# The start of a fused attention and expert layer on one core: where the first keys and queries are projected, rotated and moved, and in which order the first loads are issued

## The reference

```python
x = x + attention(layernorm(x), wq, wk, wv, wo)   # 32 heads of 64, 8 key/value heads, rotary, causal
x = x + experts(layernorm(x), gate, w0, w1, w2)   # 8 experts of width 512, the best 2 for each token
```

```python
q, k = rope(q), rope(k)                  # x * cos + rotate_half(x) * sin
probs = softmax(where(causal, q @ k.T / 8, min))
o = probs @ v
return o.reshape(b, s, NH * HD) @ wo.T
```

## Time and profile before

| | us |
|---|---|
| median of the runs | 823.74 (823.67 to 824.26, 3 runs) |
| the profiled execution | 824.96 |
| its span, first to last instruction | 823.0 |

### The profile page before, as it was taken

The page is one execution under the profiler, slowest core; times in us unless marked ns, Lnnn a source line. Parts: engine busy times, 40 slices in busy tenths (PEclk is TensorE's granted clock), DMA queues, the critical chain, the costliest instruction groups (busy, mean ns, idle before and its releaser), DMA issues.

```text
span 823.0 us, 19373 instructions
## 1 busy us (share of the span) xinstructions
PE 759.4 (92%) x5952; PEld 646.7 (79%) x5952; DVE 509.8 (62%) x2098; ACT 479.9 (58%) x1537; POOL 420.8 (51%) x674
## 2 busy tenths in 40 slices
PE   3689999999999999999999999986598999999994
PEld 2578887988888888889888888875477778888883
DVE  5788677767666757757766767776545754333331
ACT  2477876776777777677677777656244442222220
POOL 0456664656565555556465665542314454555442
PEclk9899999999999999999999999988999999999998
DMA  6432122212202302131221221218832222222330
GB/s 195 141 113 94 51 74 61 65 40 66 75 31 61 78 32 65 42 72 42 64 69 41 65 72 33 53 43 295 292 115 44 45 49 46 47 41 45 53 51 6
DMA packets 52851, 61.05 MB, mean 74 GB/s; under 512 B 10544, under 2 KB 45616, under 8 KB 52752
## 3 DMA queue, kind: packets, MB, share of 16 engines
q1 hardware_dynamic: 45264, 50.46, 21.1%
q0 software_dynamic: 7488, 9.36, 6.7%
HBM read 26.21 MB, written 9.32 MB: 43 GB/s over the span
## 4 chain that ended last, share of the span: by engine, by line
PE 76%; DVE 11%; ACT 5%; issue 4%; DMA 2%; SPq 1%; POOL 0%; POOLq 0%; DVEq 0%; ACTq 0%
PE h L1505 13%; PE projected L379 10%; PE attn_out L524 10%; PE probsT L484 9%; PE scores L471 8%; PE yb L1524 8%; PE heads_out L503 5%; PE projected L400 3%; PE heads_out L506 2%; PE tg L1515 2%; PE projected L357 2%; ACT exps L596 2%; ACT exps L594 1%; DMA raw<-w_attn 1%; PE tx L1497 1%
## 5 line engine op out<-in xcount | busy, mean ns | idle before, releaser
L898 POOL TENSOR_SCALAR probs<-exps,inv_sums 128x128 f32<-128x128 f32 x256 | 97.9, 382 | 227.8 <-DVE inv_sums L729 180.9
L603 ACT COPY pT<-probsT 128x384 f32<-128x384 f32 x256 | 121.7, 476 | 85.2 <-PE probsT L484 85.1
L484 PE MATMUL probsT<-identity,probs 128*128 128x128 f32 x768 | 132.1, 282 | 13.3 <-ACT pT L603 12.4
L594 ACT ACTIVATE exps<-masked,neg_max 128x128 f32<-128x128 f32 x256 | 102.8, 402 | 61.2 <-DVE neg_max L723 61.1
L596 ACT ACTIVATE exps<-masked,neg_max 128x256 f32<-128x256 f32 x256 | 127.2, 497 | 0.0
L899 POOL TENSOR_SCALAR probs<-exps,inv_sums 128x256 f32<-128x256 f32 x256 | 123.0, 480 | 0.0
L1715 POOL DMA_INDIRECT out<-y,to_token x39 | 61.9, 1586 | 110.8 <-DVE y L1645 90.8
L379 PE MATMUL projected<-xT_hi,w 128*128 128x256 f32 x512 | 112.7, 301 | 5.9 <-DVE k_sin L711 3.6
L1505 PE MATMUL h<-experts_w,xsT_hi 128*128 x312 | 108.9, 431 | 4.7 <-issue 3.3
L484 PEld LDWEIGHTS probsT<-identity,probs 128*128 128x128 f32 x768 | 88.9, 143 | 27.5 <-POOL probs L899 15.5
L723 DVE CUSTOM_DVE_ANT_0 masked<-scores,tables 128x256 f32<-128x256 f32 x256 | 107.5, 420 | 0.2 <-issue 0.2
(11 more groups left out here) (179 smaller groups left out, 1627.5 us busy)
## 6 DMA issues: line engine op xcount, KB each, us to landing
qT<-rotated SPq DMA_DIRECT2D x256, 64.0 KB, 2.1
kT<-k_cos SPq DMA_DIRECT2D x64, 128.0 KB, 3.3
experts_w<-w_in SPq DMA_DIRECT2D x16, 512.0 KB, 5.8
raw<-w_attn SPq DMA_DIRECT2D x20, 256.0 KB, 3.2
experts_w_out<-w_out SPq DMA_DIRECT2D x8, 512.0 KB, 7.1
out<-x_all SPq DMA_DIRECT2D x8, 256.0 KB, 2.3
xn_rows<-raw SPq DMA_DIRECT2D x8, 256.0 KB, 3.3
x_all<-x SPq DMA_DIRECT2D x1, 1792.0 KB, 11.4
```

The costliest lines, as they stand in the source:

```text
L484: mm = nc.tensor.transpose(p_bank[:, at:at + P], probs[:, h, at:at + P], ident[:, :])
L594: nc.scalar.activation(exps[:, h, 0:P], masked[:, h, 0:P], ACT.Exp, bias=neg_max[:, h, 0:1], scale=-1.0, accum_out=sums[:, h, 0:1])
L603: nc.scalar.copy(pT[:, n % 2, h, :], p_bank[:, 0:3 * P]).then_inc(pT_done, 1)
L898: nc.gpsimd.tensor_scalar(probs[:, h, 0:P], exps[:, h, 0:P], inv_sums[:, h, 0:1], 1.0, ALU.mult, ALU.mult)
```

## The change

- `project_q` and `rope_q` take the bank as an argument. The first turn's queries go to `y_bank`, the second's to `o_bank`; PE's waits for `k_parts` and `q_parts` between the first three projections go. The first `next_q` waits for `k_parts` in place of the second `q_parts`, since the keys are now what was last in `x_bank`.
- SP issues pieces 0 and 1 ahead of the tables. The four DMAs of the first keys leave SP for ACT (`move_first_keys`), between ACT's casts of pieces 3 and 4. SP moves the first queries before it loads pieces 4 and 5, not after.
- ACT casts piece 2 after `x_hi`, not before.
- DVE multiplies the first queries by the tables ahead of the split of piece 2; three (not four) tiles' statistics stand between that and the second queries, piece 3 is split right behind them, and eleven (not seven) tiles' statistics come after.
- PE multiplies the identity by itself, into `scores0`, whose content nobody reads: 9 times between the arrival of the identity and the transposes, 7 times between the transposes and the keys.

```diff
         sp.dma_start(ident[:, :], t["ident"]).then_inc(r["ident_in"], 16)
+        load_piece(0)
+        load_piece(1)
         sp.dma_start(tables[:, :], t["attn_consts"]).then_inc(consts_in, 16)
-        for i in range(SLOTS):
-            load_piece(i)
+        load_piece(2)
+        load_piece(3)
         sp.dma_start(x_all[:, TT:TILES, :], x_dram[:, TT:TILES, :]).then_inc(x_rest_in, 16)
-        move_k(0, 0)
+        move_q(0, 0, True)
         load_piece(SLOTS)
         load_piece(SLOTS + 1)
-        move_q(0, 0, True)
         move_q(1, 1, True)
...
-                    pe.wait_ge(q_parts, 2)
+                    pe.wait_ge(k_parts, 1)
...
+        def keep_busy(n):
+
+            for i in range(n):
+                nc.tensor.matmul(s_bank[0][:, 0:P], ident[:, :], ident[:, :], start=True, stop=True)
+
         pe.wait_ge(r["ident_in"], 16)
+        keep_busy(9)
         x_transposes(0)
+        keep_busy(7)
         project_k(0, 0)
-
-        pe.wait_ge(k_parts, 1)
-        project_q(0, 0)
-
-        pe.wait_ge(q_parts, 1)
-        project_q(0, 1)
+        project_q(0, 0, bank=y_bank)
+        project_q(0, 1, bank=o_bank)
...
-        for i in range(3):
-            split_w(i)
+        def move_first_keys():
+
+            act.wait_ge(k_rotated, 1)
+            for a in range(2):
+                for copy in range(2):
+                    at = copy * HD + a * 32
+                    act.dma_start(kT[at:at + 32, 0, :, :], k_cos[:, a, :]).then_inc(k_in[0], 16)
+
+        split_w(0)
+        split_w(1)
         x_hi(0)
+        split_w(2)
         split_w(3)
+        move_first_keys()
         split_w(4)
...
         rope_k(0, 0)
+        rope_q(0, True, y_bank)
         split_w(2)
 
         dve.wait_ge(x_rest_in, 16)
-        for i in range(TT, TT + 4):
+        for i in range(TT, TT + 3):
             nc.vector.bn_stats(stats[:, i, :], x_all[:, i, :])
-        rope_q(0, True)
-        for i in range(TT + 4, TT + 7):
+        rope_q(1, False, o_bank)
+        split_w(3)
+        for i in range(TT + 3, TT + 7):
             nc.vector.bn_stats(stats[:, i, :], x_all[:, i, :])
-        rope_q(1)
-        split_w(3)
         for i in range(TT + 7, TILES):
```

More of the change, by code:

```diff
@@ L366, in weights_split, with project_q @@
             return kept(kind, i)
-        def project_q(b, g, first=0, end=12):
+        def project_q(b, g, first=0, end=12, bank=x_bank):
             hi, lo = kept("q", g)
@@ L378, in project_q @@
                 at = k * 2 * P + a * P
-                mm = nc.tensor.matmul(x_bank[:, a * SEQ:(a + 1) * SEQ], part[:, at:at + P], x[:, b % 2, k, :],
+                mm = nc.tensor.matmul(bank[:, a * SEQ:(a + 1) * SEQ], part[:, at:at + P], x[:, b % 2, k, :],
                                       start=(i % 6 == 0), stop=(i % 6 == 5))
@@ L691, in x_lo, with rope_q @@
                                     xT_hi[:, b % 2, :, :].bitcast(F32), ALU.subtract).then_inc(xT_lo_done, 1)
-        def rope_q(m, first=False):
+        def rope_q(m, first=False, bank=x_bank):
             dve.wait_ge(q_ps, m + 1)
@@ L697, in rope_q @@
                 dve.wait_ge(q_rotated, m)
-            halves = x_bank[:, :].rearrange("p (a t) -> p a t", a=2)
+            halves = bank[:, :].rearrange("p (a t) -> p a t", a=2)
             nc.vector.tensor_tensor(by_cos[:, :, :], halves, cos, ALU.mult)
```

## The result

| | before | after |
|---|---|---|
| median of 12 runs, us | 823.70 (821.90 to 825.14) | 819.34 (815.56 to 821.54) |
| the profiled execution, us | 824.96 | 818.58 |
| its span, us | 823.0 | 816.7 |

The ratio of the runs is 0.9949, 95% interval 0.9934 to 0.9964: 4.2 us faster, by the interval 3.0 to 5.4 (the medians themselves are 4.4 apart). 819.3 had been forecast. The two profiled executions differ by more, 6.4 us, and the single runs of the changed kernel spread over 6 us. Part of both goes with TensorE's clock: of the twelve runs the fastest (815.56) had the highest mean granted clock, 0.982, and the three slowest (821.27, 821.27, 821.54) the lowest, 0.970. What else is in the spread isn't known, since a trace is kept of one run only.

The account below looks back on a forecast made before the run. PE bounds the later attention; at the start engines wait for one another, along DVE's path to first maxima and SP's to piece 6. Both meet 4.4 us earlier: 823.74 - 4.4 = 819.3 us median (820.5 profiled), range 817.0 to 822.4.

Parts of the forecast that it names:

- The two paths and where they meet: Start: DVE up to first maxima, SP up to piece 6; they meet at the third queries' rotation, 4.4 us earlier.
- The clock's rise: PE before the keys: unbroken work from 3.74 brings 2.4 GHz near 9.6, so keys begin at 10.7.
- The price of an identity product: PE around the transposes: 0.43 us each at 1.2 GHz (0.54 at most), 0.215 at 2.4 GHz.
- The x load: Big x load ahead of DVE's later statistics: keeps its place in the queue and lands by about 15.5.
- The landing of piece 6: Load that ACT casts before the second exponentials: issued at 23.15, landing at 25.95, 4.6 us earlier.
- The collision of DMAs: First queries' move sharing DMA engines with the keys' last DMA: nothing taken; scores at 21.1, 1.7 us later at no cost.
- Weights ahead of tables: First loads: pieces 0 and 1 there by 7 at the latest instead of 8.53, tables by 9.5.
- +/-1.5 for stretches at 1.2 GHz: Later slow-clock stretches, each some 1.5 us of PE, may vanish or appear; counted only in the range.
- rival C: Later 1.2 GHz stretches fall otherwise: one goes, 817.7 us, or one is added, 820.9; chance 0.10 each.
- Rival A: PE stays at 1.2 GHz because near-zero products don't raise the clock; 0.35 us later, 824.1; chance 0.06.
- Rival B: Clock falls in PE's gap before the second queries, which take 2.94 us, 1.2 more; 820.5 us; chance 0.15.
- Rival D: Keys' and queries' DMAs collide or issues are dear on ACT; 820.2 us, or 822.2 if transfers hold; chance 0.07.

Follow-up runs that it names:

- the fastest version: Changed kernel with piece 6 issued ahead of the second queries' DMAs and PE's waits filled with identity products; median 816.47 against 823.28 us, ratio 0.9922.
- the second set of runs: The changed kernel run again with no edit, for a second trace; median 820.10 against 823.60 us for the kernel before, ratio 0.9953.
- the first filled kernel: Changed kernel with more identity products in PE's waits (15, 12 and 4); median 817.63 us, ratio 0.9930 to the kernel before.
- that with nine products: Changed kernel without the seven identity products between transposes and keys, the nine ahead kept; ratio 0.9968 to the kernel before.
- one moved line: Changed kernel with SP issuing piece 6 ahead of the second queries' four DMAs, not behind; median 818.97 against 823.28 us, ratio 0.9942.
- the three kernels with filled waits: Changed kernel with extra identity products in PE's waits: alone (817.63 us), with piece 6 earlier (816.47), and that with keys' DMAs on SP (816.83).

## Why the prediction came out right, point by point

- *The two paths and where they meet* held. The chain went through piece 6, DVE was late next. First maxima were forecast for 24.25 and came at 23.17; piece 6 for 25.95 and was cast at 26.37; the third queries for 27.8 and came at 28.00. The sum was 4.4 for 4.20 and 4.04. That it fits so well is in part luck: 1.1 of the 4.4 are keys that begin at 10.7 and not at 11.80, and the 11.80 comes from the one late landing of piece 0 in the trace of before.
- *The clock's rise* was put near 9.6. It came by 7.8 in one trace and after 8.7 in the other, so the keys began at 9.90 and about 10.7. The price of an identity product, 0.215 at 2.4 GHz and 0.43 at 1.2, was right within the last one's tail (nine took 4.21 where the clock was 1.2 GHz throughout and 3.79 where it rose within them, seven 1.73). The sum there has a slip: with four of seven at 2.4 GHz the seven would end at 11.2; a rise at 9.6 leaves 5.7 of them at the higher level and gives the 10.8.
- *The x load* I had land by 15.5, with no one waiting. It landed at 15.9 and DVE waited 0.99 for it, which cost 0.2 at most, since the second queries were on PE until 16.7. The clock's early gain of 0.8 was still there when their rope began (16.93 for 17.75) and when SP issued piece 6 (22.46 for 23.15).
- *The landing of piece 6* was taken as 2.80, from one row. It took 3.88 in the first trace, and that is where the early gain went; in the second it took 2.85, after an issue 0.5 later than forecast. Two misses of opposite sign brought both traces to 28.0 and 28.16.
- *The collision of DMAs*, priced at nothing with 1.7 us of slack, cost about 0.9: the first queries were issued at 16.11, 0.8 ahead of the forecast, and the scores began 5.09 after that and not 4.15, at 21.20, where 21.1 was forecast. The slack covered it.
- *Weights ahead of tables* was argued from one trace's landing, and in other traces of the old order the landing was 1.3 to 1.5 earlier. The step was sound as a bound but worth nothing in the traces with the change. Likewise the move of the keys to ACT: I credited it as the thing that lets SP start, and in the changed kernel it is worth 0.1 to 0.2 of start at most (1.2 in the fastest version, where SP is later). Had I priced each part by itself, I would have been wrong on both; they were covered by each other in the sum.
- *"+/-1.5 for stretches at 1.2 GHz, in the range and not in the sum"* is what decides the single run. In the profiled execution rival C happened, 1.68 us in the lower direction, and the profiled time was 818.58 where 820.5 was forecast. The median came out at 819.34. That over twelve runs the kernel before and the changed one both have their share of such stretches is likely but not shown, as eleven of the twelve have no trace. The agreement with 819.3 to 0.04 us is luck within some 1 us: the second set of runs gave 3.5 us rather than 4.4.
- *Rival A* (products of a nearly empty matrix don't raise the clock) fell with the 0.66 us transposes. *Rival B* (the clock is down again for the second queries) did not occur in the first trace of the changed kernel. It did in part in the second (2.3 us), with the keys on SP (2.6), with the tables first and in the first filled kernel, and fully in that with nine products: it deserved more than its 0.15, though the 1.2 it was priced at reached the third queries only as 0.2 to 0.7. That it is one thing with the stretches of rows 7 is not borne out: PE had waited 2.82 us ahead of the one at 33.2, but at most 1.22 in the 6 us ahead of that at 43.4. *Rival D* was true in kind and hidden.

Priced by undoing one at a time, the parts are: DVE's order 2.8, identity products 1.7 (of them 0 to 0.7 the last seven), banks 1.2, keys on ACT 0.1, tables 0.1. Each is the difference of single traces, and the two of the changed kernel are 0.16 apart, so the last two can't be told from nothing. They add to more than 4.2; several lead through the same step.

## What to carry to other kernels

When a change moves a short start of a long kernel, read its size at a point of the trace (here the third queries and the fifth turn), not from the total: the total carries clock luck as large as the effect. But such a point is measured against a trace too: take a second trace of the kernel before, which is missing here. Idle waits of TensorE near the start are worth filling with products whose result nobody reads, if the count is chosen so that they end before the next real work; and once a wait is filled or removed, the load behind it (piece 6 here) and its place in the issuing queue should be looked at at once, as one moved line gave 1.3 us more of start (though nothing yet at the fifth turn or in the median). And a landing time from one trace is one draw: for what hangs on it, take a bound.

## What the runs showed that I had not expected

- TensorE's clock came up at different times in executions of one program: with the nine products running from 3.7 us on, the transposes at 7.8 took 0.66 us in one and 1.11 in another, and the keys' tables step followed 0.8 us apart (11.69 and 12.50).
- A wait's length doesn't settle what the clock does: after the same 1.98 us of idling the second queries took 1.7, 2.3 and 2.6 us in three traces with the same PE work ahead of them, and 2.97 with seven products fewer. The granted clock fell at 20.5, 16.6, 15.9 and 15.4 in them; with the 1.7 it was still up when they ended.
- Each 3.4 us at 1.2 GHz between the third queries and the fifth turn goes with some 1.3 us lost there, where PE isn't even busy throughout: none, one and two of them gave 2.6 to 2.8, 1.2 to 1.7 and -0.1 to 0.5 us in fourteen traces. In the changed kernel's first trace the 6.8 us from 20.5 to 27.4 are at 1.2 GHz too, and DVE waited for the scores nowhere.
- Up to the first recorded change, which comes between 15.4 and 26.4 us (in one trace after 500), the granted clock reads 1.00 in every trace, also where 12 matmuls took 3.0 us (without identity products, at 10.53) as they do at 0.50. Ahead of the first recorded change the column says nothing.
- A single DMA issue on SP took 1.33 to 1.63 us instead of 0.6 in the first queries' move, in the three kernels with filled waits and in none of the nine others. The cause stays open.
